# A two-layer transformer kernel: its routed experts moved from every batch to one pass at the end, on sorted tokens

## The chip, the cores and the metric

The kernel runs on one core of a Trainium2 chip. The metric is the device time of one execution in microseconds. TensorE (PE) does the matmuls and transposes, VectorE (DVE) and ScalarE (ACT) read their results from PSUM, GpSimd (POOL) works on SBUF and issues some transfers, and SyncE (SP) issues most of the DMAs. Every engine runs its instructions in program order and waits on semaphores for the others.

## The reference, cut to what matters

```python
x = L0_attn_x                                  # (8, 512, 128)
xn = _layernorm(x)
x = x + attn0(xn, w_qkv, w_out, b_out) + fp4_ffn(xn, w_gate, w_up, w_down)
xn = _layernorm(x)
x = x + attn1(xn, Wq..bo) + moe(xn, Wr1, br1, Wr2, br2, Ws1.., We1.., We2..)
```

Both attentions have 16 heads of 8 and a softmax over all 512 tokens of the batch. The feed-forward part of layer 0 rounds its operands to a 4-bit grid in blocks of 16 with a scale for each block. The part of layer 1 is a mixture of experts:

```python
logits = relu(xf @ Wr1 + br1) @ Wr2 + br2      # 8 experts
tg, ti = top_k(softmax(logits), 2)
tg = softmax(tg / 2)
out = silu(xf @ Ws1 + bs1) @ Ws2 + bs2         # the shared expert
for e in range(8):                             # I = 512 hidden values
    h = silu(xf @ We1[e] + be1[e]) @ We2[e] + be2[e]
    w = sum(tg * (ti == e), axis=-1)           # zero for 6 of the 8 experts of a token
    out = out + w[:, None] * h
```

There are 4096 tokens, and each has two routed experts.

## The kernel before

All work is done batch by batch: 8 batches of 512 tokens, four blocks of 128 tokens each. What the next batch needs is prepared within the turn of the present one (`turn`, written out once for each engine; the order of the four lists must agree, since all waits count uses of banks).

**Attention.** Queries and keys are split into three bf16 parts, whose products are summed in one contraction of 64 rows; they pass through DRAM to be stacked (`store_parts`, `load_stacks` on SP). For the softmax a maximum of each query's scores is needed before: `maxima` computes scores with queries as rows into a pair of PSUM banks (L1039), and VectorE reduces them (L743 a pair of heads at a time, L747 one). The maxima are transposed, split in two bf16 rows and loaded as additional rows of the queries (`max_rows`, `load_max_rows`, L396), so that the second product (`score_pair`, L1091) has them subtracted. ScalarE takes the exponential from PSUM (L563), and `weighted_sums` (L1083) multiplies it by values and ones. A slot is one block of 128 keys with four heads: two score pairs, two exponentials, four products of weighted sums. A batch has 16 slots for each layer.

**Experts.** In layer 1 the shared expert and all 8 routed ones run on all 512 tokens: in each of 9 x 4 chunks a hidden product (`expert_hidden`, L970, 512 columns), ScalarE's silu (L605), and four output products of 128 tokens each (`expert_out`, L1141). VectorE adds each expert's output with the token's weight, which is zero where it wasn't chosen (`add_expert`, L831). Maxima of both layers are put between the chunks and between the slots of layer 1's attention.

**PSUM.** 8 banks: two for single results (`ring`), two for sums (`sums`), and two pairs for scores and maxima (`mx`). Three buffers hold exponentials.

**Other steps.** Layer normalisation: VectorE's statistics (L660 to L665), GpSimd's power (L452), VectorE's application (L671). GpSimd computes residuals with biases (L457, L464) and the third bf16 part (L470), and issues the output's DMA (L475). VectorE copies the sums out of PSUM (L766). SP loads x of the next batch, stores the parts, loads the stacks and the rows of maxima, in this order in each turn.

## Time and profile before

| | |
|---|---|
| median of 3 timed runs | 1603.03 us (1602.05 to 1603.96) |
| span of the profiled execution, first to last instruction | 1599.7 us |
| of the profiled execution's time outside the span | not recorded in the profile; the median is 3.3 us above the span |
| TensorE busy | 92% of the span |
| VectorE busy | 69% |
| ScalarE busy | 51% |
| GpSimd busy | 6% |
| mean granted TensorE clock | 0.964 of full |
| DMA | 87.71 MB, mean 55 GB/s |

A group of the profile is all instructions of one line, engine, operation and tile; its busy time counts overlapping instructions once. In the timeline the first column is the start in us from the span's beginning, the second how long the (merged) instructions took; `PEld` is the loading of a matmul's stationary operand. An fp32 matmul has two records, a bf16 one has one. Waits are named by the instruction that ended them.

### The profile page before, as it was taken

The numbers are of one execution on the slowest core, as the hardware profiler recorded it, in microseconds if no ns is written. First come the engines' busy times: TensorE is split into PE (matmuls) and PEld (weight loads), VectorE is DVE, ScalarE is ACT, GpSimd is POOL, SyncE is SP. The second block draws the span as 40 slices with busy tenths as digits, with TensorE's granted clock in tenths as the row PEclk, the third lists the DMA queues.
The fourth block names the chain that finished last, engine by engine and source line by source line (L and its number), as shares of the span: only waits on it lengthen the run. The fifth ranks groups of instructions, "written<-read, shape, count | busy, mean of one in ns | idle before, by whom it ended". The sixth has DMA issues, their size and how long they took to land.

```text
span 1599.7 us, 22035 instructions
## 1 busy us (share of the span) xinstructions
PE 1465.1 (92%) x8221; PEld 659.9 (41%) x8253; DVE 1111.6 (69%) x2019; ACT 822.7 (51%) x1007; POOL 102.6 (6%) x138
## 2 busy tenths in 40 slices
PE   2589999999999999999999999999999999997997
PEld 1124552345523553245532455234542355323551
DVE  8976884778756797667957588477875679653660
ACT  1164238742476426753278423874258542784346
POOL 5001000110001100010001100001000100001000
PEclk7689999999999999999999999999999999998998
DMA  3404200241002400034001420024100340001300
GB/s 115 162 19 148 78 2 8 73 127 45 2 15 91 129 19 2 15 119 119 2 1 44 146 62 2 8 77 132 37 2 15 103 124 12 2 8 34 85 1 8
DMA packets 93981, 87.71 MB, mean 55 GB/s; under 512 B 12889, under 2 KB 93090, under 8 KB 93618
## 3 DMA queue, kind: packets, MB, share of 16 engines
q1 hardware_dynamic: 92258, 83.59, 17.3%
q0 software_dynamic: 672, 2.16, 0.5%
q8 instruction: 66, 1.08, 0.3%
q10 hardware_dynamic: 944, 0.54, 0.1%
q14 instruction: 41, 0.34, 0.1%
HBM read 45.87 MB, written 39.85 MB: 54 GB/s over the span
## 4 chain that ended last, share of the span: by engine, by line
PE 69%; DVE 16%; ACT 10%; issue 3%; DVEq 2%; POOL 1%; ACTq 0%; POOLq 0%
PE ring L970 17%; PE sums L1141 15%; PE mx L1091 11%; PE sums L1083 11%; ACT ex L563 9%; DVE nm L743 8%; PE mx L1039 6%; PE ring L976 3%; PE ring L965 2%; DVEq L825 2%; PE ring L1039 2%; DVE macc L831 2%; PE ring L1018 1%; DVE xn L671 1%; DVE att L777 1%
## 5 line engine op out<-in xcount | busy, mean ns | idle before, releaser
L563 ACT ACTIVATE ex<-mx 128x1024 f32<-128x1024 f32 x512 | 497.6, 1027 | 149.8 <-PE mx L1091 148.7
L743 DVE TENSOR_REDUCE nm<-mx 128x2 f32<-128x1024 f32 x428 | 501.3, 1217 | 85.3 <-PE mx L1039 81.1
L605 ACT ACTIVATE ex<-ring,b_sb 128x512 f32<-128x512 f32 x288 | 197.0, 687 | 418.7 <-PE ring L970 418.6
L1141 PEld LDWEIGHTS sums<-w_sb,ex 128*128 128x128 f32 x2304 | 283.5, 191 | 94.6 <-issue 91.8
L1141 PE MATMUL sums<-w_sb,ex 128*128 128x128 f32 x2304 | 319.3, 283 | 0.1
L970 PE MATMUL ring<-xnT,w_sb 128*128 128x512 f32 x576 | 296.1, 599 | 1.7 <-ACT ex L605 1.7
L1091 PE MATMUL mx<-qs,ks 74*128 74x512 bf16 (+1 forms) x992 | 275.1, 385 | 18.4 <-ACT ex L563 6.7
L1083 PE MATMUL sums<-ex,vs 128*18 128x512 f32 x2048 | 269.0, 600 | 0.4 <-ACT ex L563 0.4
L1091 PEld LDWEIGHTS mx<-qs,ks 128*128 128x128 bf16 (+1 forms) x1024 | 71.7, 97 | 269.2 <-ACT ex L563 236.8
L1039 PE MATMUL mx<-ks,qs 64*128 64x512 bf16 x856 | 150.5, 399 | 33.8 <-DVE nm L743 33.6
L747 DVE TENSOR_REDUCE nm<-ring 128x1 f32<-128x512 f32 x168 | 108.3, 686 | 72.5 <-PE ring L1039 72.1
L1039 PEld LDWEIGHTS mx<-ks,qs 64*128 64x128 bf16 x856 | 34.1, 94 | 218.4 <-issue 127.8
L831 DVE SCALAR_TENSOR_TENSOR macc<-sums,w,macc 128x128 f32<-128x128 f32 x288 | 81.2, 345 | 37.7 <-PE sums L1141 31.2
L970 PEld LDWEIGHTS ring<-xnT,w_sb 128*128 128x128 f32 x576 | 87.7, 191 | 22.7 <-ACT ex L605 8.4
L766 DVE COPY work<-sums 128x512 f32<-128x512 f32 x32 | 22.0, 688 | 81.9 <-PE sums L1083 81.9
L1083 PEld LDWEIGHTS sums<-ex,vs 128*18 128x18 f32 x2048 | 35.3, 96 | 93.2 <-issue 90.9
L475 POOL DMA_DIRECT2D out<-macc x8 | 6.4, 799 | 1008.5 <-DVE macc L783 1008.5
L470 POOL TENSOR_TENSOR parts<-qk_f,parts 128x512 bf16<-128x512 f32 x32 | 36.4, 1157 | 223.7 <-DVE parts L683 223.7
L736 DVE TENSOR_TENSOR acc<-acc,ring 128x512 f32<-128x512 f32 x8 | 5.5, 687 | 52.7 <-PE ring L1018 52.7
L965 PE MATMUL ring<-ident,xn 128*128 128x128 f32 x64 | 12.5, 328 | 27.4 <-DVE xn L671 27.4
L516 ACT COPY hqT<-ring 128x512 f32<-128x512 f32 (+1 forms) x40 | 22.7, 593 | 21.7 <-PE ring L965 21.7
L1039 PE MATMUL ring<-ks,qs 64*128 64x512 bf16 x168 | 32.8, 387 | 0.0
(135 smaller groups left out, 1017.5 us busy)
## 6 DMA issues: line engine op xcount, KB each, us to landing
scratch<-parts SPq DMA_DIRECT2D x64, 384.0 KB, 4.0
ks<-scratch SPq DMA_DIRECT2D x256, 64.0 KB, 2.2
qs<-scratch SPq DMA_DIRECT2D x256, 64.0 KB, 2.2
scratch<-parts SPq DMA_DIRECT2D x32, 256.0 KB, 4.3
w_sb<-w SPq DMA_DIRECT2D x2, 2304.0 KB
rest<-parts SPq DMA_DIRECT2D x32, 128.0 KB, 3.2
x_sb<-x SPq DMA_DIRECT2D x8, 256.0 KB, 2.8
out<-macc POOLq DMA_DIRECT2D x8, 256.0 KB, 2.8
```

The lines of the kernel that those rows point to most:

```text
L563: act.activation(ex[:, ex_buffer(l, k), 2 * i:2 * i + 2, :], mx[bank][:, :, :], ACT.Exp, scale=SCALE).then_inc(mx_free[bank], 1)
L605: act.activation(ex[:, e % 2, c, :], bank[:, :], ACT.Silu, bias=b1_sb[:, e * EC + c:e * EC + c + 1]).then_inc(free, 1)
L743: dve.tensor_reduce(nm[l][:, t, h:h + 2], mx[bank][:, :, :], AX.X, ALU.max, negate=True).then_inc(mx_free[bank], 1)
L747: dve.tensor_reduce(nm[0][:, t, h:h + 1], bank[:, :], AX.X, ALU.max, negate=True).then_inc(free, 1)
L831: last = dve.scalar_tensor_tensor(macc[:, t, :], acc[bank][:, t * P:(t + 1) * P], w9[:, t, e:e + 1], macc[:, t, :], ALU.mult, ALU.add)
L965: last = pe.transpose(bank[0:cols, t * P:(t + 1) * P], src(t), ident[:, :])
L970: pe.matmul(bank[0:rows, 0:width], lhsT, rhs, start=True, stop=True).then_inc(full, 1)
L976: last = pe.matmul(bank[:, t * width:(t + 1) * width], src[:, t * P:(t + 1) * P], w, start=True, stop=True)
L1039: return pe.matmul(bank, qs[l][r, h, t * P:(t + 1) * P], ks[l][r, h, :], start=True, stop=True)
L1083: last = pe.matmul(acc[bank][32 * j:32 * j + 2 * VW, :], values[:, start:start + 2 * VW], ex[:, ex_buffer(l, k), j, :], start=q == 0 and s ...
L1091: return pe.matmul(bank, ks[l][r, h, s * P:(s + 1) * P], qs[l][r, h, :], start=True, stop=True)
L1141: last = pe.matmul(acc[bank][:, t * P:(t + 1) * P], ex[:, e % 2, c, t * P:(t + 1) * P], w2_sb[:, e, c, :], start=c == 0, stop=c == EC - 1)
```

## The change

**Routed experts.** They no longer run in the turns. In each batch the router's two choices give every token two places in a DRAM table `xsort`, which has a region of 4096 rows for each expert. Its place within the region is a running count: matmuls with a triangular matrix rank the tokens (`ranks`, `places`). GpSimd scatters the normalised tokens there with 8 indexed DMAs a batch (`scatter`). After the last batch VectorE computes a table of 39 tiles of 256 rows (each expert's count rounded up to whole tiles), and for each tile GpSimd fetches the expert's weights (128 rows of 4112 bytes) and twice 128 token rows by index; TensorE transposes them, multiplies, and SP stores the tile's result in `ysort`. At the end GpSimd fetches both results of every token (64 indexed DMAs of 128 rows), and VectorE adds them with their weights to what the batch had (`base`, stored to DRAM and loaded again) (`combine`). The table `xsort` is first filled with zeros: 16 DMAs of 1 MB, 16.8 MB in all, on SP's queue ahead of the first rows of maxima. The shared expert stays in the turns (`shared_hidden`, `shared_out`), with the bias products of all experts added in its sums.

**Order of the turns.** A batch has two turns of 16 slots. Turn A of batch b: layer 0's scores and exponentials of batch b with layer 1's maxima of batch b-1. Turn B of b: layer 1's scores of b-1 with layer 0's maxima of b+1. All other work has a slot and a place in it (`work_a`, `work_b`): "a" after the first score pair, "b" after the second, both ahead of the maxima; "c" on VectorE after its reductions. Exponentials and sums of layer 1 thus come a batch later than before. Turn A of b = 8 has the first 16 tiles; tiles 16 to 38 follow, then the last 16 slots of layer 1's attention with no maxima.

**Maxima.** They use only four of the eight blocks of the stacked rows: 32 rows for a head, four heads side by side on the 128 rows (`qm`, `km`), loaded from DRAM by themselves before the third part is stored (`store_early`, `load_max`, `store_late`). All are reduced two heads at a time.

**Banks.** One ring bank (two before), one for sums (two), three pairs (two); two buffers of exponentials (three). Gate and up products go to pairs and cover two token blocks; the quantisation of the hidden values works on two blocks at once.

**Engines.** The application of the normalisation moves from VectorE to GpSimd (`normalize`), the copying of the sums from VectorE to ScalarE (`sums_out`).

The core of the diff; VectorE's and ScalarE's lists have the same slots as TensorE's, and in addition VectorE does at place "c" of turn A: statistics of layer 0 (slot 0), quantisation of the hidden values (1, 2, 3 and 5, 6, 7), splitting of queries and keys (4), router weights (8), quantisation of x (10, 11, 13).

```diff
-NRING, NACC, NMX = 2, 2, 2
-NEX = 3
+SLOTS = 16
+NEX = 2
+NMX = 3
...
+            def maxima(l, b, u):
+                g, t = u // NT, u % NT
+                if t == 0:
+                    pe.wait_ge(max_in[l][g], (b + 1) * N_MAX)
+                for i in range(2):
+                    bank, full = to_pair(("M", l, b, u, i))
+                    for j in range(2):
+                        r = slice(32 * (2 * i + j), 32 * (2 * i + j) + 32)
+                        done = pe.matmul(bank[:, j, :], qm[l][r, g, t * P:(t + 1) * P], km[l][r, g, :], start=True, stop=True)
+                    done.then_inc(full, 1)
...
+            def score_pair(l, b, k, i):
+                if i == 0 and k % 8 == 0:
+                    pe.wait_ge(stack_in[l][k // 8], (b + 1) * N_STACK)
+                    pe.wait_ge(rows_in[l][k // 8], (b + 1) * N_ROWS)
+                bank, full = to_pair(("E", l, b, k, i))
+                for j in range(2):
+                    h, t = head(k // NT, 2 * i + j), k % NT
+                    r = score_rows(h % 2)
+                    done = pe.matmul(bank[:, j, :], ks[l][r, h, t * P:(t + 1) * P], qs[l][r, h, :], start=True, stop=True)
+                done.then_inc(full, 1)
...
+            def tile_in(i):
+                pe.wait_ge(xg_in[i % 2], (i // 2 + 1) * 32)
+                bank = to_ring(("T", i))
+                for h in range(2):
+                    done = pe.transpose(bank[:, h * P:(h + 1) * P], xg[i % 2][:, h * P:(h + 1) * P], ident[:, :])
+                done.then_inc(ring_full, 1)
+            def tile_hidden(i):
+                pe.wait_ge(w_in[i % NW], (i // NW + 1) * 16)
+                ring_read(pe, ("T", i))
+                bank, full = to_pair(("TH", i))
+                for c in range(EC):
+                    done = pe.matmul(bank[:, c // 2, c % 2 * TS:(c % 2 + 1) * TS], wbuf[i % NW][:, c * P:(c + 1) * P], xgT[i % 2],
+                                     start=True, stop=True)
+                done.then_inc(full, 1)
+            def tile_out(i):
+                pair_read(pe, ("TH", i))
+                bank = to_ring(("TO", i))
+                for h in range(2):
+                    for c in range(EC):
+                        done = pe.matmul(bank[:, h * P:(h + 1) * P], hm[i % 2][:, c, h * P:(h + 1) * P],
+                                         wbuf[i % NW][:, FE + c * P:FE + (c + 1) * P], start=c == 0, stop=c == EC - 1)
+                done.then_inc(ring_full, 1)
...
+            def work_a(b, k, place):
+                at = (k, place)
+                if b <= LAST:
+                    if at == (0, "a"):
...
+                    if at == (12, "a"):
+                        ffn_down(b)
+                if b + 1 <= LAST:
+                    if at == (1, "b"):
+                        norm0(b + 1)
+                    if at == (3, "a"):
+                        q0(b + 1)
...
+                    if b - 1 < LAST:
+                        if at == (4, "b"):
+                            router_hidden(b - 1)
+                        if at == (5, "b"):
+                            router_logits(b - 1)
+                        if at == (9, "b"):
+                            ranks(b - 1)
+                        if at == (11, "b"):
+                            gates_transposed(b - 1)
+                    if at == (6, "b"):
+                        shared_hidden(b - 1, 0)
+                        shared_hidden(b - 1, 1)
+                    if at == (9, "a"):
+                        max_rows(1, b - 1, 0)
+                    if at == (12, "b"):
+                        shared_out(b - 1)
...
+            def work_b(b, k, place):
+                at = (k, place)
+                if b >= 1 and at == (0, "a"):
+                    max_rows(1, b - 1, 1)
+                if at == (2, "a"):
+                    sums_transposed(0, b, 0)
+                if at == (2, "b"):
+                    sums_transposed(0, b, 2)
+                if at == (4, "a"):
+                    attention_transposed(0, b)
+                if at == (5, "a"):
+                    attention_out(0, b)
+                if at == (8, "a"):
+                    norm1(b)
+                if at == (9, "a"):
+                    q1(b)
+                if at == (9, "b"):
...
+                    if at == (1, "a"):
+                        v0(b + 1)
+                    if at == (6, "a"):
+                        quantized_x(b + 1)
+                    if at == (7, "b"):
+                        gate_pair(b + 1, 0)
+                        gate_pair(b + 1, 1)
+                    if at == (8, "b"):
+                        up_pair(b + 1, 0)
+                    if at == (10, "b"):
+                        up_pair(b + 1, 1)
+                    if at == (10, "a"):
+                        max_rows(0, b + 1, 0)
...
+            def turn_a(b):
+                for k in range(SLOTS):
+                    if b <= LAST:
+                        score_pair(0, b, k, 0)
+                    else:
+                        flush_sums()
+                    work_a(b, k, "a")
+                    if b <= LAST:
+                        score_pair(0, b, k, 1)
+                    work_a(b, k, "b")
+                    if b >= 1:
+                        maxima(1, b - 1, k)
+                    flush_sums()
+                    if b <= LAST:
+                        pending.append((slot_of(0, b, k), 0, b, k))
+                    else:
+                        tile_step(k)
+            def turn_b(b):
+                for k in range(SLOTS):
+                    if b >= 1:
+                        score_pair(1, b - 1, k, 0)
+                    else:
+                        flush_sums()
+                    work_b(b, k, "a")
+                    if b >= 1:
+                        score_pair(1, b - 1, k, 1)
+                    work_b(b, k, "b")
+                    if b + 1 <= LAST:
+                        maxima(0, b + 1, k)
+                    flush_sums()
+                    if b >= 1:
+                        pending.append((slot_of(1, b - 1, k), 1, b - 1, k))
+            def tile_step(i):
+                if i == 0:
+                    tile_in(0)
+                if i + 1 < NTILE:
+                    tile_in(i + 1)
+                if i < NTILE:
+                    tile_hidden(i)
+                if i >= 1:
+                    tile_out(i - 1)
...
+            def normalize(l, b):
+                src = x_sb if l == 0 else x1
+                pool.wait_ge(var_ready[l], b + 1)
+                pool.tensor_tensor(rstd[l][:, :], veps[l][:, :], minus_half[:, :], ALU.pow).then_inc(rstd_ready[l], 1)
+                pool.wait_ge(rstd_ready[l], b + 1)
+                if b >= 1:
+                    if l == 0:
+                        pool.wait_ge(xq_ready, b)
+                    else:
+                        pool.wait_ge(scattered, 16 * 8 * b)
+                    ring_read(pool, (f"xT{l}", b - 1))
+                for t in range(NT):
+                    done = pool.tensor_scalar(xn[l][:, t, :], src[:, t, :], mv[l][:, t, 0:1], rstd[l][:, t:t + 1], ALU.subtract, ALU.mult)
+                done.then_inc(xn_ready[l], 1)
...
+            def scatter(b):
+                pool.wait_ge(pos_ready, b + 1)
+                if b == 0:
+                    pool.wait_ge(zero_out, 16 * NZERO)
+                for c in range(2):
+                    for t in range(NT):
+                        pool.indirect_dma_start(out=xsort[:, :], out_offset=bass.IndirectOffsetOnAxis(ap=pos_i[:, b, c, t:t + 1], axis=0),
+                                                in_=xn[1][:, t, :], in_offset=None).then_inc(scattered, 16)
+            def fetch_weights(i):
+                if i >= NW:
+                    pool.wait_ge(ring_full, ring.at(("TO", i - NW))[1] + 1)
+                pool.indirect_dma_start(out=wbuf[i % NW], out_offset=None, in_=wmoe[:, :],
+                                        in_offset=bass.IndirectOffsetOnAxis(ap=w_idx[:, i:i + 1], axis=0)).then_inc(w_in[i % NW], 16)
+            def fetch_tokens(i):
+                if i >= 2:
+                    pool.wait_ge(ring_full, ring.at(("T", i - 2))[1] + 1)
+                for h in range(2):
+                    pool.indirect_dma_start(out=xg[i % 2][:, h * P:(h + 1) * P], out_offset=None, in_=xsort[:, :],
+                                            in_offset=bass.IndirectOffsetOnAxis(ap=x_idx[:, i, h:h + 1], axis=0)).then_inc(xg_in[i % 2], 16)
...
+            def fetch_results(b):
+                if b >= 2:
+                    pool.wait_ge(summed, b - 1)
+                for c in range(2):
+                    for t in range(NT):
+                        pool.indirect_dma_start(out=yb[b % 2][:, c, t, :], out_offset=None, in_=ysort[:, :],
+                                                in_offset=bass.IndirectOffsetOnAxis(ap=y_idx[:, b, c, t:t + 1], axis=0)).then_inc(yb_in[b % 2], 16)
...
+            for i in range(NZERO):
+                sp.dma_start(xsort[i * 16 * P:(i + 1) * 16 * P, :].rearrange("(p r) c -> p (r c)", p=P),
+                             hs[:, :, :].rearrange("p c t -> p (c t)")).then_inc(zero_out, 16)
+            load_rows(0, 0, 0)
...
-                for e in range(NE):
-                add_expert(part, it, NE - 1)
```

## Rows read from the trace of the kernel before

**Rows 1.** The page's busy times and shares of the span by engine:
```profile
PE 1465.1 (92%) x8221; PEld 659.9 (41%) x8253; DVE 1111.6 (69%) x2019; ACT 822.7 (51%) x1007; POOL 102.6 (6%) x138
```

**Rows 2.** The page's chain of waits, shares of the span by engine:
```profile
PE 69%; DVE 16%; ACT 10%; issue 3%; DVEq 2%; POOL 1%; ACTq 0%; POOLq 0%
```

**Rows 3.** Groups by line: busy us, mean ns of one, idle us before:
```profile
L743 DVE TENSOR_REDUCE nm<-mx 128x2 f32<-128x1024 f32 x428 | 501.3, 1217 | 85.3 <-PE mx L1039 81.1
L747 DVE TENSOR_REDUCE nm<-ring 128x1 f32<-128x512 f32 x168 | 108.3, 686 | 72.5 <-PE ring L1039 72.1
L831 DVE SCALAR_TENSOR_TENSOR macc<-sums,w,macc 128x128 f32<-128x128 f32 x288 | 81.2, 345 | 37.7 <-PE sums L1141 31.2 <-issue 1.6
L766 DVE COPY work<-sums 128x512 f32<-128x512 f32 x32 | 22.0, 688 | 81.9 <-PE sums L1083 81.9
...
L671 DVE TENSOR_SCALAR xn<-x,mv,rstd 128x128 f32<-128x128 f32 x32 | 13.6, 485 | 5.8 <-POOL rstd L452 5.8
...
L671 DVE TENSOR_SCALAR xn<-x_sb,mv,rstd 128x128 f32<-128x128 f32 x32 | 11.6, 525 | 1.2 <-POOL rstd L452 1.2
...
L1141 PE MATMUL sums<-w_sb,ex 128*128 128x128 f32 x2304 | 319.3, 283 | 0.1
L970 PE MATMUL ring<-xnT,w_sb 128*128 128x512 f32 x576 | 296.1, 599 | 1.7 <-ACT ex L605 1.7
```

**Rows 4.** Timeline of an expert chunk with two maxima pairs:
```profile
206.06 1.02 PE L970 MATMUL ring<-xnT,w_sb 128*128 128x512 f32 x2
...
207.02 0.60 PE L1039 MATMUL mx<-ks,qs 64*128 64x512 bf16 x4
...
207.45 2.36 DVE L743 TENSOR_REDUCE nm<-mx 128x2 f32<-128x1024 f32 x2 [0.80 <-PE mx L1039]
...
207.55 1.16 PE L1141 MATMUL sums<-w_sb,ex 128*128 128x128 f32 x8
208.44 0.30 PEld L970 LDWEIGHTS ring<-xnT,w_sb 128*128 128x128 f32 x2
```

**Rows 5.** Timeline of a slot of layer 1's attention:
```profile
242.01 1.04 PE L1091 MATMUL mx<-qs,ks 74*128 74x512 bf16 x4
...
242.71 1.94 ACT L563 ACTIVATE ex<-mx 128x1024 f32<-128x1024 f32 x2 [0.40 <-PE mx L1091]
...
243.30 1.05 PE L1083 MATMUL sums<-ex,vs 128*18 128x512 f32 x8
...
244.28 0.11 PEld L1091 LDWEIGHTS mx<-qs,ks 128*128 128x128 bf16 x2 [0.85 <-ACT ex L563]
```

**Rows 6.** Groups by line, GpSimd:
```profile
L452 POOL TENSOR_TENSOR rstd<-veps,minus_half 128x4 f32<-128x4 f32 x16 | 16.3, 1019 | 222.0 <-DVE veps L665 222.0
L464 POOL TENSOR_TENSOR macc<-x,bo_sb 128x128 f32<-128x128 f32 x32 | 13.5, 452 | 0.0
...
L481 POOL MEMSET ks<- 32x2048 f32 x6 | 11.0, 1841 | 0.3
L475 POOL DMA_DIRECT2D out<-macc x8 | 6.4, 799 | 1008.5 <-DVE macc L783 1008.5
```

**Rows 7.** Windows: length, then busy us (count) of PE, PEld, DVE, ACT, POOL, clock, DMA share, GB/s:
```profile
140.00:148.00 8.00, 5.58 (x20) 3.10 (x18) 5.15 (x9) 1.15 (x2) 3.41 (x9) 0.79 0.35 99
120.00:124.00 4.00, 3.78 (x24) 1.19 (x28) 2.23 (x4) 4.00 (x6) 0.00 (x0) 1.00 1.01 341
```

**Rows 8.** Timeline of the startup:
```profile
56.26 0.43 SPq L426 DMA_DIRECT2D w_sb<-w  x1
...
69.70 0.45 POOL L457 TENSOR_TENSOR acc<-x_sb,bo_sb 128x128 f32<-128x128 f32 x1 [38.58 <-DMA w_sb<-w]
...
85.32 1.02 ACT L563 ACTIVATE ex<-mx 128x1024 f32<-128x1024 f32 x1 [33.96 <-PE mx L1091]
```

**Rows 9.** Timeline at the router, VectorE and GpSimd side by side:
```profile
341.93 1.16 POOL L470 TENSOR_TENSOR parts<-qk_f,parts 128x512 bf16<-128x512 f32 x1 [9.53 <-DVE parts L683]
...
342.49 0.64 DVE L795 TENSOR_TENSOR le<-lsort 128x32 f32<-128x32 f32 x1
```

More of the change, by code:

```diff
@@ new lines, in from_ring, with from_pair, copy_out, values0 @@
+            def from_ring(name):
+                act.wait_ge(ring_full, ring.at(name)[1] + 1)
+                return ring_bank
+            def from_pair(name):
+                p, before = pairs.at(name)
+                act.wait_ge(mx_full[p], before + 1)
+                return mx[p], mx_free[p]
+            def copy_out(name, dst, rows=P, width=T):
+                bank = from_ring(name)
+                act.copy(dst, bank[0:rows, 0:width]).then_inc(ring_free, 1)
+            def values0(b):
+                bank = from_ring(("v0", b))
+                wait(act, pv_done, slot_of(0, b - 1, SLOTS) if b else 0)
+                act.copy(vs[0][:, :, :, VW:VW + HD].rearrange("p t h d -> p (t h) d"),
+                         bank[:, :].rearrange("p (n d) -> p n d", d=HD)).then_inc(ring_free, 1)
@@ L645, in _ @@
-            turn(B - 1, "last")
+            act.copy(wdT[0:FC[2][1], 2, :], bank[0:FC[2][1], 2 * P:3 * P]).then_inc(ring_free, 1)
+            copy_out(("xqT", 0), xqT[:, :])
+            gates(0, 0)
+            gates(0, 1)
+            act.wait_ge(weights_in, 16 * N_WEIGHT_DMAS)
+            for b in range(B):
+                turn_a(b)
+                turn_b(b)
+            turn_a(B)
+            for i in range(SLOTS, NTILE):
+                tile_hidden(i)
+            for k in range(SLOTS):
+                if k == 9:
+                    sums_out(1, LAST, 0)
+                exponentials(1, LAST, k, 0)
+                exponentials(1, LAST, k, 1)
@@ L923, in _ @@
                 dve.memset(vs[l][:, :, :, VW + HD:2 * VW], 1.0)
[L924 to L925 removed]
+            dve.memset(acc[:, :], 0.0).then_inc(acc_free, 1)
             dve.memset(w9[:, :, 0:1], 1.0).then_inc(vec_set, 1)
[L927 to L928 removed]
+            dve.wait_ge(consts_set, 6)
+            dve.tensor_copy(upper[:, :], upper_f[:, :])
+            dve.memset(ones[:, :], 1.0)
```

1878 lines of the change are left out of this document (1009 added, 869 removed).

## The prediction

> **What bounds the kernel now.** I read the page's busy times first: TensorE 92%, VectorE 69%, ScalarE 51% [rows 1]; then the chain of waits, 69% of which runs on TensorE [rows 2]; then the groups by line. The two expert lines (hidden products 296.1 us, output products 319.3 us) are 615 us of TensorE's 1465 [rows 3]. In the timeline the matmuls of an expert chunk follow each other without a hole [rows 4], and the attention slots too [rows 5]. So TensorE bounds before, at its upper clock nearly all the time. VectorE has 609.6 us of maxima (501.3 + 108.3) and 502 us of everything else [rows 3]. The span is 1599.7; the three timed runs have a median of 1603.0, so some 3 us lie around it, and I add them at the end.
>
> **What leaves TensorE, and what comes.** Before, each batch runs 36 hidden products and 144 output products. One hidden product takes 0.96 us (206.06 to 207.02) and four output products 0.89 (207.55 to 208.44) [rows 4]: 36 x 0.96 + 36 x 0.89 = 66.6 us a batch, 533 in all. After, the shared expert stays (4 x 0.96 + 4.0 = 7.8 with its biases, 63 in all), and 39 tiles of 256 columns come: hidden 4 x 0.5 = 2.0, output 2 x 0.89 = 1.8, two transposes 0.2, so 4.0 us each, 156 in all. TensorE loses about 314 us of work. That isn't the gain: the work that stays is ordered anew, and VectorE keeps its maxima (512 reductions; before 428 double and 168 single ones). So I go through the new order.
>
> **The base slot of a phase.** Turns A and B have 16 slots; in a full slot TensorE issues score pair E0, E1, maxima pair M0, M1, sums, through three bank pairs taken in turn. M1 gets the pair that E0 had. A score pair takes 0.43; ScalarE begins 0.70 after its start (242.01 to 242.71) and reads for 0.97; the sums take 0.98 (243.30 to 244.28) [rows 5]. Two maxima pairs take 0.53 (207.02 to 207.55) and VectorE starts 0.43 after the first [rows 4]; a reduction takes 1.17 (501.3 by 428) [rows 3]. With E0 at 0, ScalarE has read it at 1.67, M1 goes at 1.7 to 2.0, the sums end at 2.98: **3.0 us a slot**, against 2.5 of matmuls. VectorE has 2.3 of maxima in it and 0.7 of room. That the maxima contract 32 rows rather than 64 is worth nothing here: TensorE waits for ScalarE's read at that place; bounds are 0 and the 0.27 of a whole pair a slot [rows 4].
>
> **VectorE's other work.** From 1111.6 I take the maxima, the weighting of experts (81.2), the sums' copies (22.0, now ScalarE's) and the normalisation (13.6 + 11.6, now GpSimd's): 373.8, of which some 35 is startup, so 42 a batch [rows 1, 3]. Joined halves in the quantisation save 3, the two extra halves of maxima rows and the places of the tokens add 5, drains between dependent operations 5: 49.5 a batch, 37.5 in A and 12 in B by the lists of the two turns.
>
> **A full turn A.** VectorE 16 x 2.34 + 37.5 = 75, and it waits beyond that: slot 0, 1.1, for the transposes of maxima rows that need the last reduction; slot 1, 3.5: its statistics go to GpSimd, whose power takes 1.02 and whose four normalising instructions 0.45 each [rows 6], 3.0 with signals, then transposes before the maxima of that slot, and all that stands behind them; slot 2, 1.0 (one ring bank between two transposes); slot 5, 1.2; slot 9, 2.9 (ScalarE's two table loads around tanh delay the score pair); slot 10, 1.2; slot 12, 6.0: down projection and shared output, 7.0 us of matmuls, stand before the maxima. Bubbles in slots with no other work 1.4. Sum 18.3: **93 us**. A full turn B: 37.4 + 12 + waits of 1.1, 1.3, 1.0, 0.5 in slots 0, 1, 2, 5, 7.2 for gate, up, q and k products (slots 7 to 10) and 4.7 for seven slots held at 3.0: **65 us**. So A and B give 158 a batch, with 124 of VectorE and some 115 of TensorE in them; neither engine is full, the order binds them.
> The clock: a hole of about 2.4 us in TensorE's work is followed by a granted clock of 0.79 over 8 us [rows 7]. Each turn A has one (slot 1); in the heavy slots after it VectorE is the slower engine at either level, 1.2 or 2.4 GHz, so I take 1 us a turn A (bounds 0 and 5).
>
> **Start.** First exponential before at 85.3 [rows 8]. New on SP's queue, ahead of the first rows of maxima: 16 writes of zeros, 16.8 MB in all. Bulk loads moved 4.7 MB between 56.3 and at most 69.7 (350 to 420 GB/s with 2 us of latency off) [rows 8]; the stores of parts saturate at 341 [rows 7]. The zeros begin at about 55 (SP had issued the stacks before 56.3), take 40 to 49 us, and the rows land behind them: first scores at **102**, 17 later.
>
> **Turns of the ends.** A of batch 0 (no maxima; exponentials 2.1 a slot, the wait of slot 1, projections): 43. B of batch 0 (maxima alone): 55. A of batch 1: 87. Then six A at 94, six B at 65, and B of batch 7 (no maxima, the router of the last batch in slots 11 to 14): 42. From 102: 102 + 43 + 55 + 87 + 564 + 390 + 42 = **1283**.
>
> **The tiles.** A tile's matmuls are 4.0, and the only ring bank must be read by VectorE between output product and next transpose, 0.8: 4.8. 23 tiles alone: 110. The first 16 stand beside the last maxima: 5.2 a slot, with 14 of shared expert, projection and rows: 97. Before the first, eight scatters, their landing and the first fetches make TensorE wait 10.
> GpSimd issues three indexed transfers a tile. The trace has none. Nearest rows: a plain one 0.80, and 1.02 for an instruction on four elements a partition; the highest GpSimd row 1.84 (a memset of 2048) [rows 6]. I take 1.1: 3.3 a tile, hidden under 4.8; at 1.84, 5.5, not hidden, +25 over all tiles. The weights, 0.53 MB a tile, take 1.6 us at 341 GB/s: hidden, 16 DMA queues being otherwise idle then.
> The Trainium skill, DMA: Bandwidth & Descriptors, Specifications, gives about 1 us to the first byte of a transfer issued by GpSimd, 0.6 from the other queues; no row here shows an indexed one. At 1.0 the sum would be 6 us lower.
>
> **The end.** GpSimd fetches 64 sorted results, after the last tile's store (4 us): 64 x 1.1 = 70, then landing, combination and store 9: **83**. Layer 1's last attention (16 x 2.16 + 7 = 42) lies beside it. Bounds 64 x 0.8 = 51 and 64 x 1.84 = 118, so -19 and +48.
> Sum: 1283 + 10 + 97 + 110 + 83 = 1583; the waits of A and B were taken one after the other, though the engines drift by up to a slot and some cover each other: I take off 1 us in each of the 13 full turns, so 1570 in the span, and 3 around it: **1573**, 30 us faster. 314 us of matmuls go, but about 17 at the start, 41 at the end beyond attention and some 220 in slots held by waits come back.
>
> **The rivals.**
> (a) The waits overlap much better: A and B together at 140, near what VectorE alone needs (124 and its gaps). For it: TensorE is at 92% before with the same kinds of waits [rows 1]. Against: one ring bank instead of two, and products placed ahead of maxima in program order. 7 x 18 less: 1450.
> (b) They overlap worse, a pair at 167: GpSimd's chain, ScalarE's table loads and the low clock [rows 7] hit slots that I priced at 3.0. 7 x 9 more: 1640, slower. It decides from 4 us more a pair.
> (c) GpSimd and VectorE hinder each other. Beside GpSimd's subtraction (341.93) VectorE took 0.64 for a 128x32 subtraction [rows 9], nearly the 0.69 of a 128x512 copy [rows 3]; a hit costs between 0 and one GpSimd instruction, 1.16 [rows 9]. After, GpSimd has some 24 instructions a batch where it had 15 and VectorE's two-input operations (quantisation, combination) are beside them; 12 hits a batch x 0.7, and twice that in the end's fetches: 8 x 8.4 + 20 = 87: 1660, slower. It decides from 30 us, four hits a batch.
> The Trainium skill, SBUF — State Buffer, SBUF: two separate sides, says it more strongly: VectorE and GpSimd share one port pair, the loser fully blocks, and GpSimd can't write its descriptors meanwhile. By that rule the trace agrees in the 0.64; how often it hits scatters no run here shows.
> (d) The indexed transfers cost 1.84 or more each: +25 for tiles, +48 at the end, +8 before: 1654, slower.
> That the selection does other work than it says (all 39 tiles are run whatever the counts) changes nothing in time: the tile count is fixed.
>
> **How the numbers follow.** Forecast as reckoned, 0.42; its own range 1535 to 1610, of which 0.33 faster, 0.04 within 0.2%, 0.05 slower. (a) 0.20. (b) 0.16, (c) 0.11, (d) 0.11. A difference of 0.2% (3 us) is about what a measurement of this kernel can tell. Faster 0.33 + 0.20 = 0.53, and 0.02 of (b): 0.55; same 0.04; slower 0.41. The range reaches to the middle of (a) and past (c): 1470 to 1675.
>
> **What would show it.** First exponential near 102, with row loads waiting behind zero writes (a start at 85: the zeros were hidden). x loads, one a batch, 158 us apart; a base slot of 3.0 between the sums of slots 13 to 15 in B; in slot 1 of A a hole on TensorE ended by GpSimd's normalisation; in slot 12 a VectorE idle of 5 to 6 us. Tiles 4.8 apart with TensorE waiting for VectorE's copy (5.5 and GpSimd never idle: rival d). After the last tile some 80 us with GpSimd issuing and TensorE idle for half of them. The forecast is wrong if a pair A and B is under 150 or over 166, or if the tiles are bound by their transfers.

## The result, and where the time went

The changed kernel takes 1662.0 us (median of 4), the kernel before 1602.8 beside it: ratio 1.036, interval 1.0345 to 1.0379. It is 59 us slower; I had forecast 1573, 30 us faster. The profiled execution has a span of 1660.9 against the forecast span of 1570, so 91 us have to be found. The stated bounds of 1470 to 1675 hold 1662 only because they reached over the rivals; the forecast's own range ended at 1610.

The page of the changed kernel (busy times as in [rows 1], the granted clock in 40 slices, the chain as in [rows 2]):

```profile
PE 1199.5 (72%) x6747; PEld 522.3 (31%) x6807; DVE 1016.8 (61%) x1596; ACT 723.0 (44%) x921; POOL 375.0 (23%) x395
...
PEclk9668668987898889878987798889989979999985
...
PE 27%; DVE 27%; issue 21%; POOL 9%; ACT 6%; DVEq 6%; DMA 3%; SPq 1%; ACTq 0%; POOLq 0%
```

TensorE lost 266 us of busy time [rows 1] and its share of the chain fell from 69% [rows 2] to 27%: no engine bounds the kernel now. I had expected 314 us less; the scores and sums that stayed run partly at the lower clock (mean granted 0.868, before 0.964), and the 2048 records of sums take 304 us where they took 269. A first look at the groups (line, shapes, count, busy us and mean ns, idle before it and its releaser):

```profile
L959 DVE TENSOR_REDUCE nm<-mx 128x2 f32<-128x1024 f32 x512 | 600.6, 1216 | 168.8 <-PE mx L329 165.5
...
L347 PE MATMUL sums<-ex,vs 128*18 128x512 f32 x2048 | 304.3, 669 | 5.0 <-ACT pv_sb L699 2.6
...
L965 DVE CAST nm_hl<-ring 8x512 bf16<-8x512 f32 x32 | 21.6, 676 | 66.1 <-PE ring L253 66.1
```

VectorE's maxima cost what they did (1216 ns for a pair, [rows 3]) and it is idle 169 us before them. The waits of TensorE that stand out (us in total, times, longest):

```profile
PE mx L359 <- DMA qs<-nm_hl: 52.6, 8, 11.3
PE ring L253 <- POOL xn L1313: 41.9, 9, 10.0
```

The first is a wait of the scores for the rows of maxima that SyncE copies. Its longest, 11.3 us, is the start, where the rows stand behind the zeros, as forecast; the other seven, 4.0 to 9.5 us each and 41 in all, come once in each turn A from batch 1 on, and no step of the prediction had them. The second is the hole in slot 1 of turn A, which the prediction did have.

The stages, from the starts of the exponentials and maxima in the trace, against my terms:

| stage | forecast | measured | difference |
|---|---|---|---|
| first scores | 102 | 99.1 | -3 |
| A0, B0, A1 | 43, 55, 87 | 49.4, 60.2, 89.2 | +14 |
| A2 to A7 | 564 | 557.8 | -6 |
| B1 to B6 | 390 | 422.8 | +33 |
| B7 | 42 | 46.5 | +5 |
| tiles, with their lead | 217 | 241.1 | +24 |
| after the tiles | 83 | 94.8 | +12 |
| deduction for waits that cover each other | -13 | 0 | +13 |

Before rounding they sum to 91. In the row A2 to A7 two errors cancel: A2 to A6 take 93.0 to 96.8 each, 6 us over in all, and A7, which prepares no further batch, takes 81.5 where I had put a full 94. A turn B of 70.4 with a turn A of 93 to 97 makes a pair of 165, seven above my 158: that is rival (b), reached by another way than the one I had named for it.

**The end of turn B.** Timeline of the changed kernel around the start of the turn A of batch 3 (start us, length, engine, line; SPq is SyncE's queue):

```profile
507.03 0.61 PE L359 MATMUL mx<-qs,ks 74*128 74x512 bf16 x2
...
509.17 0.68 DVE L967 TENSOR_TENSOR nm_hl<-ring,nm_hl 8x512 bf16<-8x512 f32 x1
...
515.97 0.40 SPq L1430 DMA_DIRECT2D scratch<-parts  x1
...
521.20 0.55 SPq L1451 DMA_DIRECT2D qm<-scratch  x1
...
526.32 0.59 SPq L1436 DMA_DIRECT2D scratch<-parts  x1
...
530.55 2.57 SPq L1469 DMA_DIRECT2D qs<-nm_hl  x4
...
534.32 1.01 PE L359 MATMUL mx<-qs,ks 74*128 74x512 bf16 x2 [5.33 <-DMA qs<-nm_hl]
```

VectorE has layer 0's rows ready at 509.85. SyncE issues their copies at 530.55: ahead of them in its list stand four stores that wait for VectorE's split in slot 10, eight loads that wait for these stores to land, and six more stores. The scores of turn A come 5.3 us late, once a turn, and run at the lower clock (1.01 for a pair that took 0.61 at 507.03).

**Slots 1 and 12 of turn A.** GpSimd's normalisation and what waits for it, then the projections of slot 12 (one turn later in the trace):

```profile
541.72 1.03 POOL L1304 TENSOR_TENSOR rstd<-veps,minus_half 128x4 f32<-128x4 f32 x1 [23.44 <-DVE veps L865]
...
542.86 3.14 POOL L1313 TENSOR_SCALAR xn<-x_sb,mv,rstd 128x128 f32<-128x128 f32 x4
...
546.05 1.11 PE L253 MATMUL ring<-ident,xn 128*128 128x128 f32 x4 [4.00 <-POOL xn L1313]
```

```profile
606.80 2.84 PE L316 MATMUL ring<-wdT,hqT 128*128 128x128 f32 x24
...
616.86 0.69 DVE L1052 TENSOR_TENSOR macc<-macc,ring 128x512 f32<-128x512 f32 x1 [6.23 <-PE ring L434]
...
617.47 2.35 DVE L959 TENSOR_REDUCE nm<-mx 128x2 f32<-128x1024 f32 x2
```

The first is as forecast, but a normalising instruction takes 0.79, not the 0.45 of the nearest row [rows 6]. The second is nearly as forecast: VectorE idle 6.2, where I had 6.0.

**After the tiles.** GpSimd's fetches at the end:

```profile
1567.39 0.95 POOL L1361 DMA_INDIRECT qs<-ysort,y_idx  x1 [14.94 <-DMA ysort<-qs]
...
1568.64 0.95 POOL L1361 DMA_INDIRECT qs<-ysort,y_idx  x1 [0.30 <-issue]
...
1646.31 0.95 POOL L1361 DMA_INDIRECT ks<-ysort,y_idx  x1 [0.30 <-issue]
```

An indexed transfer takes 0.95 and a gap of 0.30 follows: one in 1.25, 64 in 80 us. I had 1.1.

### The profile page after: what moved, and what is told of

It reads as the page before. It is cut to its first block, busy times and chain, and to the rows that moved or that the text cites. A ratio compares the mean times of both kernels' runs of the same rounds, so it can differ in the third digit from the quotient of the medians.

```text
span 1660.9 us, 18766 instructions
## 1 busy us (share of the span) xinstructions
PE 1199.5 (72%) x6747; PEld 522.3 (31%) x6807; DVE 1016.8 (61%) x1596; ACT 723.0 (44%) x921; POOL 375.0 (23%) x395
## 4 chain that ended last, share of the span: by engine, by line
PE 27%; DVE 27%; issue 21%; POOL 9%; ACT 6%; DVEq 6%; DMA 3%; SPq 1%; ACTq 0%; POOLq 0%
DVE nm L959 13%; PE sums L347 5%; ACT ex L695 3%; PE mx L359 3%; PE ring L458 3%; PE mx L329 3%; PE mx L409 2%; PE mx L449 2%; PE ring L433 2%; POOL qs L1361 2%; POOL ks L1361 2%; PE ring L253 2%; POOL xn L1313 2%; DVEq L914 1%; DVEq L873 1%
## 5 line engine op out<-in xcount | busy, mean ns | idle before, releaser
L959 DVE TENSOR_REDUCE nm<-mx 128x2 f32<-128x1024 f32 x512 | 600.6, 1216 | 168.8 <-PE mx L329 165.5
L359 PE MATMUL mx<-qs,ks 74*128 74x512 bf16 (+1 forms) x964 | 316.9, 422 | 104.0 <-DMA qs<-nm_hl 52.6
L347 PE MATMUL sums<-ex,vs 128*18 128x512 f32 x2048 | 304.3, 669 | 5.0 <-ACT pv_sb L699 2.6
L329 PE MATMUL mx<-km,qm 32*128 32x512 bf16 x1024 | 151.5, 431 | 83.2 <-DVE nm L959 54.5
L1340 POOL DMA_INDIRECT xsort<-xn,pos_i x64 | 62.7, 979 | 238.9 <-DVE pos_i L1046 221.8
L329 PEld LDWEIGHTS mx<-km,qm 32*128 32x128 bf16 x1024 | 36.9, 93 | 222.4 <-DVE nm L959 97.3
L373 PE MATMUL ring<-ident,pv_sb 128*128 128x128 f32 x128 | 21.9, 298 | 59.1 <-DVE att L975 57.6
L1353 POOL DMA_INDIRECT qs<-xsort,x_idx x40 | 37.9, 947 | 15.1 <-issue 10.4
L433 PE MATMUL ring<-w_sb,hs 128*128 128x128 f32 x256 | 36.8, 287 | 4.3 <-DVE acc L952 3.7
L1353 POOL DMA_INDIRECT ks<-xsort,x_idx x38 | 35.9, 946 | 12.4 <-issue 9.5
```

The lines of the kernel that those rows point to most:

```text
L329: done = pe.matmul(bank[:, j, :], qm[l][r, g, t * P:(t + 1) * P], km[l][r, g, :], start=True, stop=True)
L347: done = pe.matmul(acc[32 * j:32 * j + 2 * VW, :], values[:, start:start + 2 * VW], ex[:, s % NEX, j, :], start=q == 0 and t == 0, stop=q ...
L359: done = pe.matmul(bank[:, j, :], ks[l][r, h, t * P:(t + 1) * P], qs[l][r, h, :], start=True, stop=True)
L373: done = pe.transpose(bank[:, i * P:(i + 1) * P], pv_sb[:, i % 2, (t + i // 2) * P:(t + i // 2 + 1) * P], ident[:, :])
L433: pe.matmul(bank[:, t * P:(t + 1) * P], hs[:, c, t * P:(t + 1) * P], w2_sb[:, c, :], start=c == 0, stop=False)
L959: dve.tensor_reduce(nm[l][:, t, h:h + 2], bank[:, :, :], AX.X, ALU.max, negate=True).then_inc(free, 1)
```

## Experiments

All are edits of the changed kernel. A ratio is against the kernel before, measured beside it (1602.1 to 1602.6). Theory Q is that orders of queues cost the time in a few places that can be undone one by one; its rivals stand in the expectations. The edits are cut to their core, and some of their lines are in words.

### Rows ahead of the stores

```
-   store_early(1, b); load_max(1, b); store_late(1, b)
-   if b + 1 <= LAST: load_rows(0, b + 1, 0)
+   if b + 1 <= LAST: load_rows(0, b + 1, 0)
+   store_early(1, b); load_max(1, b); store_late(1, b)
```

> One edit on the changed kernel: in SyncE's list the eight-partition rows of layer 0's first half (load_rows(0, b+1, 0)) go ahead of store_early, load_max and store_late of layer 1; no work is added or removed. Theory Q (queues and orders: the lost time sits in few places where one queue's order holds all engines): at 530.55 SyncE issues these rows only after 18 other transfers, although VectorE wrote them some 20 us earlier; the first scores of turn A come at 534.3, TensorE idle 5.3 us before, and run at the lower clock after it. Seven turns A gain 5.3 plus up to 2 of clock: 37 to 50 us, so 1612 to 1625, first slot gap ahead of A near 3 and not 11. Theory H (GpSimd and VectorE hinder each other, rival c of the prediction): the wait moves to VectorE's next operation, less than 10 us: 1652 or more. Theory D (indexed transfers are too dear, rival d): nothing, 1662.

Measured 1625.9, ratio 1.0158 (1.0139 to 1.0177): 36 us less. The same place in its trace:

```profile
494.99 0.68 DVE L967 TENSOR_TENSOR nm_hl<-ring,nm_hl 8x512 bf16<-8x512 f32 x1
495.70 2.54 SPq L1469 DMA_DIRECT2D qs<-nm_hl  x4
...
514.37 1.73 SPq L1441 DMA_DIRECT2D rest<-parts  x2
...
516.14 0.11 PEld L359 LDWEIGHTS mx<-qs,ks 74*128 74x128 bf16 x2 [0.85 <-issue]
```

The copies go out 0.03 us after VectorE's instruction ended, and the first scores of turn A at 516.1 wait for nothing of DMA. From the maxima of one turn A to the next the pair falls from 164.9 (mean of six) to 159.7, against my 158. By the exponentials, turns B1 to B6 lose 30 us and the turn B of batch 0 loses 9. The lower edge of the expectation (37) was just missed: a pair gives 5.2, and nothing more for the clock.

### Statistics a turn earlier

```
-   if at == (0, "c"): norm_stats(0, b + 1)              # turn A
+   if at == (14, "c") and b + 2 <= LAST: norm_stats(0, b + 2)   # turn B
```

> One edit on the changed kernel: VectorE takes layer 0's statistics of a batch at slot 14 of the turn B before, instead of slot 0 of its turn A, so that GpSimd's power and four normalising instructions lie beside slots 14 and 15. Theory Q: in turn A TensorE waits 4.0 us (542.0 to 546.05) for the normalised rows and VectorE 5.4 us; the gap from slot 0 to slot 1 falls from 10.1 to 5 or 6. Seven turns (A0 keeps its order): 28 to 40 us, so 1622 to 1634. Theory H: GpSimd's 4.2 us then run beside two more maxima slots and lengthen VectorE's operations there; the gain is under 15 us. Theory D: nothing.

Measured 1645.4, ratio 1.0277 (1.0260 to 1.0294): 17 us less. The gap from slot 0 to 1 fell from 10.1 to 5.8 as expected, but the pair by 3.4 only, and 28 was the least I had expected: the gaps after slots 1, 2 and 9 of turn A grew by 0.2 to 0.3 each, and the last gap of turn B, which now has the statistics, from 2.8 to 3.9. 4.3 us in slot 0 are not 4.3 in the turn.

### Shared output behind the maxima

```
-   if at == (12, "b"): shared_out(b - 1)    # TensorE and VectorE
+   if at == (12, "c"): shared_out(b - 1)    # behind maxima (and sums)
```

> One edit on the changed kernel: in slot 12 of turn A the shared expert's output product (36 matmuls, 6 us) stands behind the maxima and the sums of the slot, and VectorE adds it after its maxima. Theory Q: VectorE's 6.2 us of idle before L1052 (8 times) go; TensorE's work is the same, so the slot of 11.7 becomes about 8 and one or two slots behind it (2.8 to 4.4) grow by less than 1: 2.5 to 4 us a turn, 8 turns, 20 to 30 us: 1632 to 1642. If TensorE and not VectorE bounds this stretch: nothing, 1662.

Measured 1653.6, ratio 1.0325 (1.0307 to 1.0342): 8 us less, a third of what I expected. Slot 12 shrinks from 11.8 to 5.0 and slot 13 grows from 2.8 to 8.3: the 6 us of matmuls are in one piece and hold the next slot's scores. A wait moved is not a wait gone.

### Zeros behind the rows

```
-   the 16 zero writes, then load_rows(0, 0, 0)
+   load_rows(0, 0, 0), load_rows(0, 0, 1), then the 16 zero writes
```

> One edit on the changed kernel: the 16 writes of zeros (16.8 MB) are issued after both halves of layer 0's rows of batch 0, not ahead of the first. My step of the start (they cost 17 us): the first exponential comes at 82 to 86 instead of 99, and the first shared expert, which waits for them, is 100 us away: 1645 to 1650 if nothing else waits. Rival: the stores and loads of batch 1's scores now queue behind the zeros' 45 us, and turn B of batch 0 gets the time back: 1655 to 1662.

Measured 1657.6, ratio 1.0367 (1.0331 to 1.0403), no different from the changed kernel. The first exponential comes at 88.4 instead of 99.1, and turn A of batch 0 takes 54.9 instead of 49.4: half is given back at once, the rest doesn't show beside the spread of this run (1651.7 to 1668.4). The rival's time holds, but not its place: it had put the loss into turn B of batch 0, which takes 60 us as before. My step (zeros ahead of the rows cost 17) was right in place; their price was 11, of which 5 would be paid anyway.

### Four edits together, and a fifth

> The four edits of e1 to e4 together: rows ahead of the stores, layer 0's statistics at slot 14 of the turn before, shared output behind the maxima, zeros after both rows. One by one they took off 36, 17, 8 and 4 us. Theory Q (the waits stand one after the other in the order of the turns, each can be taken away by itself): the sum, 65 us, 1597, and perhaps 5 to 15 more since fewer holes are followed by the lower clock: 1582 to 1600, at or below the kernel before. Rival S (the engines drift by up to a slot, so that one wait covers another): at most 45 us, 1617 or more.

Measured 1597.7, ratio 0.9961 (0.9948 to 0.9974): 64 us less. By the medians the four alone sum to 66, by the ratios to 51; either way nothing is lost when they come together, and rival S is out. It also speaks against my deduction of 13 us for waits that cover each other.

```
-   (5, "b"): router_logits, router_sort;   (6, "a"): router_exp
+   (6, "a"): router_logits, router_sort;   (7, "a"): router_exp
```

> As e5, and layer 1's router logits one slot later (slot 6 instead of 5, the router's exponential at slot 7). In the changed kernel TensorE waits 3.8 us in slot 5 of turn A for the ring bank that VectorE frees behind its split of 2.6 us (569.93), and the scores of slot 6 come 3 us late at the lower clock. Theory Q: the gap from slot 4 to 5 (8.7) and 5 to 6 (7.4) lose together 3 to 4 us in each of seven turns: 20 to 28 us below e5. If VectorE's work bounds these slots: within 5 us of e5.

Measured 1579.0, ratio 0.9851 (0.9834 to 0.9868): 19 us below the four, just under the 20 expected. The gap from slot 4 to 5 is 5.6 instead of 8.2. One ring bank was the cause: TensorE's logits needed the bank that VectorE would free only behind a split of 2.6 us.

### Half the fetches

```
-   for c in range(2):   # fetch_results and combine
+   for c in range(1):
```

> The changed kernel with only the first choice's results fetched and added at the end (32 indexed transfers instead of 64, 32 VectorE additions less); it leaves the second choice's results out of the output. The end stage is GpSimd's issue of 64 transfers, one in 1.25 us (0.95 and a gap of 0.30). Theory D (indexed transfers set the end): 32 x 1.25 = 40 us less, 1622, and the end stage 55 instead of 94.8, just over layer 1's last attention (42). Rival: attention or the additions set the end, then less than 20 us less.

Measured 1621.8, ratio 1.0117 (1.0100 to 1.0134): 40.2 us less for 32 transfers, 1.26 each. This kernel leaves the second choice's results out of the output, and with them 32 additions of VectorE; but VectorE does four additions in 1.14 us and then waits 3 to 5 us for the next fetches. So the end of the changed kernel is bound by the issue of the indexed transfers.

### More GpSimd work beside the quantisation

```
+   for n in range(16):
+       pool.drain()
+       pool.tensor_tensor(spare_o, bo_sb[0], bo_sb[1], ALU.add)
```

> The changed kernel with 16 more GpSimd additions (128x128, two inputs) in each turn A of seven, behind the third part of layer 0's queries and keys, so beside slots 5 to 8 where VectorE quantises; they write a buffer that nobody reads. Theory H (GpSimd and VectorE hinder each other, rival c of the prediction): each addition of about 0.45 us holds up VectorE's two-input operation beside it or is held up; 3 to 7 us a turn, 20 to 50 us more: 1682 to 1712, and the quantisation's 128x704 operations in slots 5 to 7 are longer than their 0.89. Theory Q: GpSimd is idle there and nothing waits for it: 1658 to 1668.

Measured 1665.2, ratio 1.0382 (1.0363 to 1.0401), 3 us above the changed kernel, and the two intervals overlap. GpSimd's additions, and one of VectorE's two-input operations of the quantisation in this run, then the same in the changed kernel:

```profile
L1400 POOL TENSOR_TENSOR spare_o<-bo_sb 128x128 f32<-128x128 f32 x112 | 53.7, 479 | 19.7 <-issue 4.9
...
L904 DVE TENSOR_TENSOR h_sb<-h_sb,qrs 128x704 f32<-128x704 f32 x16 | 14.5, 905 | 0.1
```

```profile
L903 DVE TENSOR_TENSOR h_sb<-h_sb,qrs 128x704 f32<-128x704 f32 x16 | 14.3, 893 | 0.1
```

54 us of GpSimd work (573.8 to 583.3 in one turn, beside the first steps of the quantisation) lengthen this operation by 12 ns on average and the kernel by 3 us, not the 20 to 50 of theory H. The average hides that only 4 of the 16 stand beside an addition: these take 0.98 us, the other 12 take 0.88. The additions did not reach the last three steps of the quantisation (588 to 591), so this run alone can't exclude a larger hit there. The trace of the changed kernel does: after the first exponential 81 of VectorE's instructions overlap a computing instruction of GpSimd, and six of them are more than 0.06 us longer than is usual in their group, 2.1 us together; GpSimd's own instructions are longer by 2.5 us in all. The two engines do hinder each other, but for under 5 us, where rival (c) had 87. It is out as the cause of the loss.

### Maxima from 64 rows

```
-   r = slice(32 * (2 * i + j), 32 * (2 * i + j) + 32)
+   r = slice(64 * i, 64 * i + 64)
```

> The changed kernel with each maxima product contracting 64 rows as before (two heads' rows together, so the maxima are those of sums of two heads; time alone is of interest). Theory of the prediction: TensorE waits at that place, 32 rows are worth nothing; 1660 to 1668. Rival L: in the base slot of 2.8 us the loop is the third pair: first maxima product of a slot waits for VectorE's last reduction of the slot before, and VectorE for it (0.49 idle and 2 x 1.18). The product pair of 64 rows ends some 0.2 later, so each slot held by this loop gets 3.0: 150 to 300 slots of 0.1 to 0.2, 20 to 50 us more, 1682 to 1712, and the gaps 2.8 in turn B read 3.0.

Measured 1681.8, ratio 1.0498 (1.0476 to 1.0520): 20 us more. A pair of maxima products and the reductions behind it in a base slot, with 32 rows (changed kernel), then with 64:

```profile
455.85 0.40 PE L329 MATMUL mx<-km,qm 32*128 32x512 bf16 x4 [0.53 <-DVE nm L959]
...
456.28 2.36 DVE L959 TENSOR_REDUCE nm<-mx 128x2 f32<-128x1024 f32 x2 [0.49 <-PE mx L329]
```

```profile
475.52 0.61 PE L329 MATMUL mx<-km,qm 64*128 64x512 bf16 x4
...
476.16 2.36 DVE L959 TENSOR_REDUCE nm<-mx 128x2 f32<-128x1024 f32 x2 [0.70 <-PE mx L329]
```

The four 32-row products start close together and VectorE waits 0.49; with 64 rows it waits 0.70, and the gaps of 2.8 read 3.0. So the base slot's loop is VectorE's two reductions and the turnaround to TensorE and back (2.35 + 0.49), not TensorE's wait for ScalarE's read, as I had it. The Trainium skill, TensorE: Matmul & The Clock Gate, Why this matters for your kernels, says that matmuls of 32 rows on different row groups run at the same time; these rows agree, and the prediction should have asked what that is worth to the engine that waits. The mean granted clock was 0.889 in this slower kernel, 0.868 in the changed one: a higher clock bought it no time.

### The normalisation on VectorE again

```
+   for t in range(NT): dve.tensor_scalar(xn[l][:, t, :], ...)   # behind rstd_ready
-   for t in range(NT): pool.tensor_scalar(xn[l][:, t, :], ...)
```

> One part of the change undone on the changed kernel: VectorE applies the normalisation again (4 instructions of 128x128), GpSimd only takes the power. GpSimd's four take 0.79 each (3.14), VectorE's took 0.49 to 0.53 before (2.0). Theory Q: the hole in slot 0 of turn A shortens by 1 us and the statistics' wait for GpSimd's power (1.2) goes onto VectorE in slot 5 of turn B, where 3.2 us more stand before the maxima: -8 and +22 over the turns, so 1668 to 1680. Theory H: VectorE is freed of GpSimd's port use and gains: under 1655.

Measured 1691.3, ratio 1.0549 (1.0530 to 1.0568): 29 us more, beyond the 18 I had as the most. VectorE's new groups:

```profile
L872 DVE TENSOR_SCALAR xn<-x_sb,mv,rstd 128x128 f32<-128x128 f32 x32 | 18.1, 720 | 9.2 <-POOL rstd L1311 9.2
L872 DVE TENSOR_SCALAR xn<-x,mv,rstd 128x128 f32<-128x128 f32 x32 | 16.5, 573 | 9.3 <-POOL rstd L1311 9.3
```

35 us of work and 18 of waiting for the power stand in VectorE's queue. A turn B grows from 69.8 to 75.2, a turn A shrinks by 0.5. Moving the normalisation to GpSimd was a good part of the change; it was put where its latency shows. The means of 0.72 and 0.57 are of two kinds of instruction. Most take 0.33; the first of the four in a turn starts just behind a GpSimd addition and ends with it:

```profile
553.88 1.26 POOL L1316 TENSOR_TENSOR acc<-x_sb,bo_sb 128x512 f32<-128x512 f32 x1
553.94 1.28 DVE L872 TENSOR_SCALAR xn<-x_sb,mv,rstd 128x128 f32<-128x128 f32 x1 [1.13 <-POOL rstd L1311]
```

There are 15 such pairs, 7 in layer 0 and 8 in layer 1, and each costs VectorE 0.95 us: 14 us, about the 11 by which the loss passed the 18 of the expectation. So the hindrance of rival (c) is real and this order of the queues invites it; the changed kernel hardly meets it.

### Ahead of the tiles, and the shared output in pieces

```
-   fetch_weights(i); fetch_tokens(i)          # GpSimd
+   fetch_tokens(i); fetch_weights(i)
-   load_stacks(1, LAST, 0 and 1) ahead of the tiles   # SyncE
+   the same behind the second tile's store
```

> As e6 (1579), and two edits ahead of the tiles: layer 1's last score stacks (16 transfers on SyncE) are loaded behind the second tile, and GpSimd fetches each tile's tokens ahead of its weights. In e6 the first slot of turn A of the tiles takes 26.1 us; the first token fetch is issued at 1331 of the changed kernel and read at 1340, with 0.27 MB of weights ahead of it and the stacks beside it. Theory Q: the lead falls by 4 to 8 us: 1571 to 1576. Rival: the tokens wait for the scatters' landing and the queue's own latency, so within 2 us of e6.

Measured 1564.3, ratio 0.9765 (0.9749 to 0.9781): 15 us less, twice the expectation. The lead falls from 26.1 to 18.4; the two edits were made together, so which of them did it isn't shown. The rest lies in the tiles; TensorE's waits for tokens in the kernel with five edits (two buffers), then in this one:

```profile
PE ring L441 <- DMA qs<-xsort,x_idx: 26.3, 9, 16.9
...
PE ring L441 <- DMA ks<-xsort,x_idx: 11.9, 9, 3.7
```

```profile
PE ring L441 <- DMA qs<-xsort,x_idx: 9.1, 1, 9.1
...
PE ring L441 <- DMA ks<-xsort,x_idx: 3.1, 1, 3.1
```

So the forecast's statement that the tiles hide their transfers held only nearly: 16 of 18 waits go once the tokens don't queue behind a tile's weights (0.53 MB; the expectation's 0.27 was my slip).

```
+   SHARE = {12: [0], 13: [1], 14: [2, 3]}
-   if at == (12, "c"): shared_out(b - 1)
+   if place == "c" and k in SHARE: shared_out(b - 1, SHARE[k])   # added in slot 15
```

> As e11, and the shared expert's output product is spread: one tile of tokens behind the maxima of slots 12 and 13, two behind those of slot 14, added by VectorE in slot 15. In e6 slots 12 to 14 take 5.0, 8.3 and 4.4. TensorE has 2.5 us of attention in a slot and VectorE 2.35: if TensorE's work alone counts, the 6 us are no longer beside idle engines but fill the 0.3 to 2 us of room in each slot: 2 to 4 us a turn, 14 to 28 us below e11: 1545 to 1560. Rival: the rows of quantised x (slots 12 and 13) and the single ring bank hold the stretch anyway: within 5 us of e11.

Measured 1546.7, ratio 0.9659 (0.9643 to 0.9675): 18 us less again. The gaps that end with the maxima of slots 12, 13, 14 and 15 take 4.9, 3.7, 4.6 and 6.1; they took 5.0, 8.3, 4.4 and 2.8. This version beats the kernel before by 55 us and the changed one by 115, with the same matmuls. Windows of one turn A and one turn B of the changed kernel, then of this one (window: length, busy us and count of PE, PEld, DVE, ACT, POOL, granted clock, DMA share, GB/s):

```profile
368.30:465.10 96.80, 74.28 (x399) 29.62 (x401) 68.39 (x119) 43.19 (x51) 15.48 (x16) 0.83 0.33 82
465.10:535.40 70.30, 52.34 (x318) 17.69 (x323) 48.51 (x56) 39.66 (x44) 7.68 (x8) 0.97 0.25 69
```

```profile
344.50:431.90 87.40, 73.68 (x403) 28.38 (x403) 68.52 (x111) 42.85 (x51) 14.21 (x15) 0.84 0.37 96
431.90:495.60 63.70, 52.44 (x320) 17.39 (x320) 47.92 (x64) 39.65 (x44) 8.69 (x9) 1.00 0.23 63
```

The busy times of PE, DVE and ACT are equal to within 1 us; 16 us of waiting are gone from the pair.

## Why the prediction failed, step by step

- **The order of SyncE's queue at the end of turn B** is the step that failed. I went through 16 slots of a turn B (65, and 65.0 is the mean turn B once the rows go first) and priced the transfers that the change adds to the start and the end; but of the rows of maxima, which now serve a turn that begins while the other layer's stores go out, I asked nothing of the queue. The prediction's own rule (what stands ahead of a step in SP's queue) was applied to the zeros alone. Price: 33 us in B1 to B6 and 5 in B0 by the table; by experiment 36 for the whole kernel. That is the larger part of the loss of 59, but less than half of the 91 that the forecast missed: without it the kernel is still 1.6% slower than before. The rest are the smaller terms below.
- **The deduction of 13 us** for waits that cover each other had no row behind it, and the table shows nothing of it. The four edits together give as much as one by one, though two of them, alone, gave less than their wait.
- **The tiles**, 24 too low: a lead of 25.9 where I had 15 with its slot (two edits together took 8 us of it away), slots beside the last maxima 6.8 on average instead of 6.1 with their extras, and 4.9 a tile alone (4.8 forecast).
- **The end**, 12 too low: a mis-sized term, 1.25 for an indexed transfer instead of 1.1, which makes 10 of the 12. That is rival (d)'s mechanism, far below its price of 1.84.
- **The full turn A** at 94 was right (93 to 97). Turn A of batch 0 is not: 49 instead of 43, with TensorE waiting 5.8 us for the normalised rows; why it waits longer there than the 4.0 to 4.5 of later turns stays open. The terms of the full turn for slot 1 and slot 12 were right in place and size of the wait. That VectorE's wait of slot 12 costs a turn 6 was wrong: 1 to 3 us of it can be had back by order, since TensorE has the work to do.
- **The base slot** of 3.0 was 2.8, and for another reason (VectorE's two reductions and the turnaround), so that the 32-row maxima, which I priced at nothing with bounds up to 0.27 a slot, are worth 20 us.
- **The clock** at 1 us a turn: the first scores behind each late row ran at the lower level (1.01 us for a pair against 0.61). The granted clock is 0.80 to 0.84 over the turns A of batches 2 to 6, and still 0.84 in the best kernel, whose turn A is 9 us shorter; the first experiment left nothing over for it. So the waits could be taken away without it, but its own part is not measured. [rows 7] also showed less than I read from it: its 8 us hold two waits, of 1.5 and 0.9 us, and not one hole of 2.4.
- **Rivals.** (b) was the nearest; it had the size (167 a pair, 165 measured) but named GpSimd, the tables and the clock, not SyncE, so its size is luck. (c) and (a) are out, (a) even after seven edits: the pair is 150 on average.
- **The sign of being wrong** was too wide: a pair of up to 166 passed as right, and the measured 165 passes, though 7 us a pair over six pairs are more than the whole gain of 30.
- **A slip** without effect: VectorE's remaining work is 373.6, not 373.8.

Open: of the 151 us of the pair in the last windows some 116 are VectorE's; what holds the other 35 was not tried (a second ring bank is the first candidate; no bank of PSUM is free for it). The gaps after slots 1, 5 and 8 of turn A (about 7, 7 and 6 us) are as in the changed kernel.

## What to carry to other kernels

When a change lets two phases overlap, write down the issue queue of each engine across the seam, DMA queues first: a short transfer that is ready early and stands behind stores that wait costs once a turn what no busy time shows. Taking work off the bounding engine bought nothing until the orders were mended; then 266 us less of TensorE's time became 55. Move long products behind the work that another engine waits for only in pieces, and give small fetches on one queue the place ahead of large ones.

## What the runs showed of the hardware

- Indexed transfers on GpSimd: on average 0.95 to 0.98 us each, and 0.30 between two that follow each other, whether scatter or gather, one row a partition of 512 bytes or of 4 KB.
- GpSimd takes 0.79 to 0.82 us for a subtract and multiply of 128x128 with two scalars a partition, 0.45 to 0.48 for an addition of that size.
- 16.8 MB of zero writes ahead of the rows cost the start 11 us, and half of that is paid again when they stand behind them.
- VectorE's two-input 128x704 operation: 0.98 us beside GpSimd's additions (4 instances), 0.88 otherwise (12 instances of the same run).
- VectorE's normalising instruction of 128x128: 0.33 us by itself, 1.28 when it starts 0.06 us behind a GpSimd addition of 1.26.
